# The relative-position line of an attention kernel: sixteen spreading transfers made thirty-two of half the length

## What is computed

```python
x = layernorm(x + L0_attn(x))          # cumulative sums over the tokens
x = layernorm(x + L0_ffn(x))           # relu(x W1[e] + b1[e]) W2[e] + b2[e], times the top probability
x = layernorm(x + L1_attn(x))          # softmax(q k^T * scale + pos_bias) v
x = layernorm(x + L1_ffn(x))           # shared and routed swiglu

# in L1_attn: the bias of a head is a function of |i - j| alone
rel = abs(r[None, :] - r[:, None]) / max(S - 1, 1)
idx = clip(round(rel * (RES - 1)), 0, RES - 1)
pos_bias = einsum('ijf,hf->hij', table[idx], Wpos)
```

## Time and profile before

| | us |
|---|---|
| median of 3 runs | 1905.35 (1903.22 to 1914.08) |
| the profiled execution, as timed | 1903.2 |
| its span in the profile | 1901.4 |
| PE busy over the span | 1715.9 |
| stage b, from the first load of `b_x` to the last store of `ys_d` | 488.1 to 598 |
| steps 10 to 25 of stage b, in which the 16 transfers are issued | 510.0 to 558.8 |

### The profile page before, as it was taken

How to read it: one execution, slowest core, us unless ns; L and a number is a source line. 1 busy time by engine, 2 the same in 40 slices (tenths; PEclk the granted TensorE clock), 3 DMA queues, 4 the chain that set the end, 5 groups by cost and what they waited for, 6 DMA issues and landing times. The chain is left out here.

```text
span 1901.4 us, 46354 instructions
## 1 busy us (share of the span) xinstructions
PE 1715.9 (90%) x15436; PEld 952.7 (50%) x15436; DVE 1322.9 (70%) x4251; ACT 1161.8 (61%) x2983; POOL 849.5 (45%) x1187
## 2 busy tenths in 40 slices
PE   7899999996576699999999999999999999399796
PEld 6477777766565133333334333343334333299554
DVE  4689999985311687878877787878877785333387
ACT  5788888873333177777777766777677767233221
POOL 0568777774433213443344333444344321422276
PEclk9999999998787599999999999999999999799898
DMA  3574434352483243343434343443434343222243
GB/s 107 176 227 163 134 132 133 127 188 91 121 198 100 80 118 105 115 128 114 139 89 129 113 133 110 113 128 116 137 87 129 109 128 86 94 84 89 84 130 94
DMA packets 150575, 231.87 MB, mean 122 GB/s; under 512 B 20485, under 2 KB 69141, under 8 KB 149797
## 3 DMA queue, kind: packets, MB, share of 16 engines
q1 hardware_dynamic: 141268, 204.54, 35.2%
q0 software_dynamic: 9072, 24.41, 4.7%
HBM read 184.25 MB, written 119.60 MB: 160 GB/s over the span
## 5 line engine op out<-in xcount | busy, mean ns | idle before, releaser
L1985 DVE CUSTOM_DVE_ANT_0 c_sums<-c_s,bias 128x512 f32<-128x512 f32 x1024 | 668.9, 686 | 189.5 <-PE c_s L1596 141.8
L1803 ACT ACTIVATE early<-c_u 128x512 f32<-128x512 f32 x1024 | 555.9, 595 | 257.2 <-PE c_u L1614 253.8
L1614 PE MATMUL c_u<-spread_line,c_pick 128*32 128x512 bf16 x4096 | 316.1, 385 | 12.6 <-DMA spread_line<-tops_d 12.6
L1628 PE MATMUL c_o<-early,c_vst 128*32 128x256 f32 x4096 | 310.9, 380 | 1.1 <-ACT early L1803 0.5
L555 ACT ACTIVATE v<-a_bank,gain 128x64 f32<-128x64 f32 x1024 | 221.4, 376 | 24.0 <-DVE vp L788 22.6
L1596 PE MATMUL c_s<-c_kst,c_qst 64*128 64x512 bf16 x1024 | 219.2, 395 | 3.2 <-DMA c_qst<-parts_d 0.8
L1604 PE MATMUL c_u<-c_qst,c_kst 64*128 64x512 bf16 x1024 | 201.9, 378 | 0.3 <-ACT early L1803 0.2
L1628 PEld LDWEIGHTS c_o<-early,c_vst 128*32 128x32 f32 x4096 | 120.2, 110 | 113.6 <-issue 17.1
L1614 PEld LDWEIGHTS c_u<-spread_line,c_pick 128*32 128x32 bf16 x4096 | 61.7, 94 | 204.6 <-issue 185.2
L407 PE MATMUL a_bank<-wv,xT 128*128 128x512 f32 x256 | 141.9, 640 | 14.2 <-ACT v L555 13.1
L1596 PEld LDWEIGHTS c_s<-c_kst,c_qst 64*128 64x128 bf16 x1024 | 52.3, 93 | 176.5 <-DVE c_tops L1985 128.3
(11 more groups left out here) (281 smaller groups left out, 2963.7 us busy)
## 6 DMA issues: line engine op xcount, KB each, us to landing
xs_d<-in_zeros SPq DMA_DIRECT2D x16, 2048.0 KB, 9.2
zs_d<-in_zeros SPq DMA_DIRECT2D x16, 2048.0 KB, 9.8
spread_line<-tops_d SPq DMA_DIRECT2D x256, 64.0 KB
parts_d<-c_parts SPq DMA_DIRECT2D x32, 384.0 KB, 5.0
c_kst<-parts_d SPq DMA_DIRECT2D x256, 48.0 KB
c_qst<-parts_d SPq DMA_DIRECT2D x256, 48.0 KB
bias_d<-line_d SPq DMA_DIRECT2D x16, 448.0 KB
bias<-bias_d SPq DMA_DIRECT2D x16, 448.0 KB, 6.1
```

What stands on the lines that cost most here:

```text
L1614: mm = nc.tensor.matmul(u_ps[bank_of(n)][ARRAY * k:ARRAY * (k + 1), :].rearrange("k (t q) -> k t q", t=T), pick[:, c, k, :], line[:, G * j ...
L1628: mm = nc.tensor.matmul(o_ps[ARRAY * i:ARRAY * (i + 1), half * 2 * P:(half + 1) * 2 * P], vst[s.par][:, c, f:f + ARRAY], pT[r % 2][:, i, h ...
L1803: nc.scalar.activation(pT[n // G % 2][:, n % G, :], u_ps[bank_of(n)][:], ACT.Exp).then_inc(sem("exp_done"), 1)
L1985: v.tensor_tensor_reduce(sums[n % 2][:], s_ps[bank_of(n)][:], bias, 1.0, -3.0e38, ALU.add, ALU.max, top_s[j % 2][:, k:k + 1]).then_inc(sem ...
```

## The change

`PIECES` goes from 4 to 8, so that a transfer covers 3,584 values (the last pieces 3,552) of 32 rows: 7,168 bytes a row, 224 KB. There are 32 of them instead of 16, with the same bytes in all. They are issued one with each of the steps 8 to 39. The new indices go through two neighbouring pieces of one group of partitions before they go on to the next group.

```diff
                 def line_spread(n):
 
                     LAST = LINE - ARRAY
-                    k, a = n // (LINE_PARTS + 1), n % (LINE_PARTS + 1)
+                    k, a = n // 2 // (LINE_PARTS + 1) * 2 + n % 2, n // 2 % (LINE_PARTS + 1)
                     first, past = LINE // PIECES * k, min(LINE // PIECES * (k + 1), LAST)
...
-                PIECES = 4
+                PIECES = 8
                 SPREADS = PIECES * (LINE_PARTS + 1)
...
-                        if 10 <= s.b < 10 + SPREADS:
-                            line_spread(s.b - 10)
+                        if 8 <= s.b < 8 + SPREADS:
+                            line_spread(s.b - 8)
```

## The result

The change makes the kernel 0.41% faster: median 1900.3 us against 1909.2 us, 15 runs each, ratio 0.9959 with a 95% interval of 0.9944 to 0.9974. One run of the kernel before (5627 us) and one of a kernel further down (2015 us) were slow, and every ratio leaves them out. The gain is 7.8 us (5.0 to 10.7), where 17 were forecast. The sign was right, the size under half of what was said, and the median lies 1.3 us outside the range. The range stood on a base of 1905.35 us, the median of three runs; the other 14 runs of the kernel before have a median of 1908.0. So it is the gain that was wrong, and only in part the base.

A forecast was written before the change was run, and what follows sets the result against it. PE was taken to stand in stage b for late loads, as DMA demand of 2.66 us a block exceeded the 1.975 pace. Winning 24.0 us less 7 gave 17: 1905.35 - 17 = 1888 us, range 1881 to 1899.

The forecast's parts named there:

- The pattern of every fourth block: In stage b, the late load was to strike every fourth block, eight times over 32 steps.
- Part (1): Stage b's DMA demand falls to 1.71 us a block against a pace of 1.975; the 24.0 us of lumps go.
- Part (2): In stage b, even blocks' loads land about 0.9 us late, eight times: 7 us lost, 0 to 15 at the bounds.
- The clock: PE's clock in stage b: nothing counted, as it stayed 1.00 after an idle of 0.88 us in the first stage.
- Parts (3) to (5): Sixteen more POOL issues (8 us, in gaps), step 8's wait (at most 0.5), the end (at most 1): cost 0.
- A: Rival for stage b: the load slips through, stalls under 0.4 us, 0 to 3 us lost, 1881 to 1884 us; chance 0.16.
- B: Rival for stage b: the transfer queue stands all the time, stalls rise towards 15 us, 1891 to 1900 us; chance 0.13.
- C: Rival for stage b: short stalls drop PE to 1.2 GHz, 12 us more, gain of 5, 1900 us; chance 0.07.
- D: Rival: slower, as a half transfer holds the DMA engines as long as a full one, 1.90 us; 1915 us; chance 0.04.

The follow-up runs named there:

- a kernel further down: Kernel before (16 full transfers) with SyncE's stores two steps later: 1892.8 us, ratio 0.9948 (median of three runs, without that of 2015 us).
- the long lead: Changed kernel with SyncE storing each pair of result blocks two steps later, so loads go out earlier: 1881.8 us, ratio 0.9867 to the kernel before.
- T3: Theory that packet length delays loads; run: changed kernel, two runs of 1,792 values a row instead of one of 3,584; 14.6 us lost.

## Why the prediction was half right

**What bounds, and why.** Right: PE stands for the load of an even block, whose lead is 2.2 us. With the lead at 5.8 us the loss is 0.0 us, with the same transfers. The pattern of every fourth block came as said.

**Part (1), the demand.** Right in its terms: 0.85 us a half transfer (0.95 said); with q1's 36.3% of 70 us, 25.4 us over the 28 blocks from 505.4 to 574.7, 0.91 a block (0.76 said), the demand is 1.76 us (1.71 said). That no backlog builds at the pace is shown by the long lead's 249 GB/s with PE at 100%. But the 24.0 us to be won were read from one execution. The mean of two is 22.8, and 3.1 of it stay even with no transfers.

**Part (2), what is late next: this is the step that failed.** It put each critical load 0.9 us late, landing at 3.05 us, behind one half transfer, eight times: 7 us. Nine were late, by 1.36 us in the mean, plus one fall of the clock and small pieces: 15.1 us in one profile, 18.1 in the other. Landings reached 4.8 and 5.2 us in these two. The median of 4.1 us in the kernel with the long lead shows it without the stalls' breaks, at 88% occupancy of the DMA engines (45.1% and 43.0%): 2.0 us over the quiet landing, where one half transfer ahead would add 0.95. As I read it, a load waits not only for the one thing issued just ahead of it but for what is left of stores, loads and transfers before it; no run shows these parts singly. I had this as the upper bound (1.90 us, 15 us in all) and took the middle, on issue times alone. At that bound the sum gives 1903.2 - 24.0 + 15 = 1894 against its own execution, and 1896 for a median. That is still 4 us short of the 1900.3 measured, against a base that itself came out 2.6 us higher.

**The clock.** Nothing was counted for it. In the first profile of the changed kernel it fell once, after an idle of 2.41 us, and that cost 1.7 us; the window from 545 to 550 us:

```profile
545.00:550.00 5.00, 5.00 (x25) 0.66 0.32 92
```

In the second profile it fell behind two stalls, at blocks 10 and 22 (idle 2.90 and 2.69 us).

**Parts (3) to (5).** Right, and shown by the long lead's 0.0 us with all of them in place: 16 more issues, POOL's wait for `lparts_d` (1.67 us there, 1.28 in the changed kernel), and the last two transfers. From the turning of block 38 to stage c on POOL it takes 8.24 us before (590.39 to 598.63) and 8.23 now.

**The rivals.** A is out. B comes nearest in its size (stalls towards 15 us, 1891 to 1900), but not by its mechanism: the queue does not stand all the time, since the same demand is met at full pace. C happened at one stall in one profile and at two in the other. D is out at 0.85 us a transfer. So the cause of the smaller gain is shown as landing times against a short lead: the long lead alone takes the loss of the changed kernel to 0.0. What within the DMA queues makes up the 3.0 to 4.8 us of one load is not: the order of pieces is out, packet length (T3) is untested, and the store ahead of the load was moved behind it only together with other loads.

## What to carry to other kernels

Compare a load's landing time under the load that the change will bring with its lead, which is the time from issue to use; that the mean demand fits is only the first of two conditions. Here an occupancy of 88% meant twice the quiet landing time in the middle and nearly three times at most. And look in the issuing queue for a wait that holds loads back: here moving the stores back by two steps won another 0.9% on top of the change (0.9867 against 0.9959 of the kernel before), over twice what halving the transfers won. In the kernel before, with its denser transfers, it won 0.5%. And read a loss from two profiles before building a sum on it.

## What the hardware showed

- Loads of 128 KB landed in 2.1 us in the quiet stretch, and in 4.1 us in the middle (5.8 at most) in a total traffic of 249 GB/s that the engines carried without falling behind.
- SP's own DMA issue, 0.34 to 0.38 us as a rule, took up to 3.05 us in the kernel with full transfers on even steps (at most 1.19 and 1.33 us in the two profiles of the changed kernel); what stands behind it goes out later.
- Splitting each row of 7,168 bytes into two runs of 3,584 bytes of one transfer left 32 packets a transfer, as many as before.
- The same kernel's stage b lost 15.1 and 18.1 us in two profiles, and 24.7 and 20.9 in the two of the kernel before.
